# Adapter stage of a two-layer adapter network: base weight split in sixteen halves at the end of a step, and y copied ahead of the second half of the next x

## The reference, cut to what matters

```python
# x: (64, 64, 1024), two layers
x = x + L0_ffn(einsum('bct,bcd->bdt', x, W0[id0]))          # layer 0
def L1_cond(x, weight, ids):                                 # one of 16 adapters for each of 64 batches
    return einsum('bij,bkj->bik', x, weight[ids])            # y = x @ weight[id].T, 1024 x 1024
def L1_ffn(y):
    base_out = einsum('bsi,oi->bso', y, base_w) + base_b     # the base weight, 1024 x 1024
    res_hidden = einsum('bsi,ri->bsr', y, A)                 # rank 64
    # router over 16 experts, the best two, gates from a softmax
    delta = einsum('bse,bsr,eor->bso', combine, res_hidden, B)
    return base_out + 0.5 * delta
x = x + L1_ffn(L1_cond(x, L1_cond_weight, id1))              # layer 1
```

## Time and profile before

| | us |
|---|---|
| median of 3 runs | 1214.57 |
| lowest and highest | 1213.8, 1217.22 |
| profiled execution, its own time | 1211.74 |
| its span | 1210.1 |
| PE busy, DVE busy, ACT busy, POOL busy | 1115.4, 689.7, 504.9, 221.0 |
| granted PE clock, mean | 0.977 |

### The profile page before, as it was taken

The page is one execution under the profiler, slowest core; times in us unless marked ns, Lnnn a source line. Parts: engine busy times, 40 slices in busy tenths (PEclk is TensorE's granted clock), DMA queues, the critical chain, the costliest instruction groups (busy, mean ns, idle before and its releaser), DMA issues.

```text
span 1210.1 us, 22388 instructions
## 1 busy us (share of the span) xinstructions
PE 1115.4 (92%) x5799; PEld 921.9 (76%) x5800; DVE 689.7 (57%) x1307; ACT 504.9 (42%) x1019; POOL 221.0 (18%) x352
## 2 busy tenths in 40 slices
PE   4989969988999899999999899989999899999997
PEld 4979958867888677777887778767676678888885
DVE  2877863472554728364555386735444366666655
ACT  1101213562654638363556471134444344444443
POOL 1021110020110202010111000054444042323220
PEclk8989979998999999999999999999999999999998
DMA  5488764493573828475665333169999799999995
GB/s 203 162 325 279 268 237 128 129 319 129 183 267 105 323 77 306 134 250 193 215 222 189 124 98 104 64 220 363 369 351 282 280 377 353 341 355 336 358 344 202
DMA packets 115051, 289.38 MB, mean 239 GB/s; under 512 B 17202, under 2 KB 21810, under 8 KB 112946
## 3 DMA queue, kind: packets, MB, share of 16 engines
q1 hardware_dynamic: 85088, 184.91, 42.9%
q0 software_dynamic: 29056, 102.38, 25.5%
q10 hardware_dynamic: 850, 1.39, 0.4%
HBM read 184.79 MB, written 103.84 MB: 239 GB/s over the span
## 4 chain that ended last, share of the span: by engine, by line
PE 65%; DVE 13%; DMA 9%; issue 7%; ACT 3%; SPq 2%; DVEq 1%; ACTq 1%; another core or an unknown queue 0%; POOLq 0%; POOL 0%
PE psum L1344 14%; PE psum L1346 14%; PE psum L1345 14%; PE psum L1529 3%; PE psum L1428 3%; DMA delta_scratch<-dl 2%; PE psum L1530 2%; PE psum L1420 2%; PE psum L1538 2%; PE psum L1355 2%; PE psum L1446 2%; DMA xp<-act_scratch 2%; PE psum L1448 2%; DMA rawb<-baseT 2%; DVE x1g L985 2%
## 5 line engine op out<-in xcount | busy, mean ns | idle before, releaser
L1344 PE MATMUL psum<-base_hi,xp_hi 128*128 128x512 f32 x512 | 204.2, 399 | 2.5 <-ACT nat L757 1.5
L1344 PE MATMUL psum<-w,xp_hi 128*128 128x512 f32 x448 | 185.5, 414 | 19.8 <-DVE xp_lo L1035 17.2
L1345 PE MATMUL psum<-base_lo,xp_hi 128*128 128x512 f32 x512 | 200.8, 392 | 0.0
L1346 PE MATMUL psum<-base_hi,xp_lo 128*128 128x512 f32 x512 | 200.7, 392 | 0.0
L1346 PE MATMUL psum<-w,xp_lo 128*128 128x512 f32 x448 | 180.0, 402 | 0.0
L1345 PE MATMUL psum<-w,xp_hi 128*128 128x512 f32 x448 | 179.8, 401 | 0.0
L583 POOL DMA_DIRECT2D raw<-w1T x112 | 59.3, 529 | 461.8 <-DVE w L1014 461.3
L1014 DVE TENSOR_TENSOR w<-raw,w 128x1024 fp32r<-128x1024 f32 x112 | 132.1, 1218 | 5.5 <-ACT w L696 3.5
L749 ACT ACTIVATE xp_hi<-xp 128x256 fp32r<-128x256 f32 x124 | 51.4, 416 | 179.4 <-PE psum L1346 137.8
L1116 DVE TENSOR_TENSOR xp_lo<-xp,xp_hi 128x256 fp32r<-128x256 f32 x124 | 51.9, 424 | 117.9 <-ACT xp_hi L749 95.2
L1344 PEld LDWEIGHTS psum<-w,xp_hi 128*128 128x128 f32 x448 | 85.7, 191 | 42.6 <-issue 24.8
(11 more groups left out here) (263 smaller groups left out, 1912.6 us busy)
## 6 DMA issues: line engine op xcount, KB each, us to landing
raw<-w1T POOLq DMA_DIRECT2D x120, 512.0 KB, 5.6
delta_scratch<-dl SPq DMA_DIRECT2D x80, 512.0 KB
xp<-act_scratch SPq DMA_DIRECT2D x74, 256.0 KB, 2.8
act_scratch<-yT SPq DMA_DIRECT2D x72, 256.0 KB, 4.7
xg<-xT SPq DMA_DIRECT2D x16, 1024.0 KB, 7.4
act_scratch<-x1g SPq DMA_DIRECT2D x16, 1024.0 KB, 5.1
x1t<-act_scratch SPq DMA_DIRECT2D x64, 256.0 KB
out<-x1t SPq DMA_DIRECT2D x64, 256.0 KB
```

The lines of the kernel that those rows point to most:

```text
L1344: mm(out, a_hi, b_hi, start=start, stop=False, skip_group_check=True)
L1345: mm(out, a_hi, b_lo, start=False, stop=False, skip_group_check=True)
L1346: return mm(out, a_lo, b_hi, start=False, stop=stop, skip_group_check=True)
```

## The change

The buffer `rawb` becomes two parts of 512 columns. The base weight comes in sixteen halves (`PARTS` = 2 KC = 16, `HALF` = 512 columns), one in each of steps 0 to 15. Part n goes to home n % 2. On ACT and DVE the base split moves from ahead of the first half of the next x to the end of the step, behind weight chunks 6 and 7. The copy of y moves ahead of the second half of the next x on both engines. SP's wait for `base_lo_done` now is for the part before the last one, and it also waits for the last part to have landed.

```diff
-            rawb = sb(s, "rawb", [P, D])
+            rawb = sb(s, "rawb", [P, 2, HALF])
@@ SP
-            sp.dma_start(rawb[:, :], baseT[0, :, :]).then_inc(rawb_in, 16)
+            sp.dma_start(rawb[:, 0, :], baseT[0, :, 0:HALF]).then_inc(rawb_in, 16)
...
                 load_pair(j + 2)
-                with sp.If(j < KC - 1):
-                    chunk = baseT[bass.ds(nc.s_assert_within(j + 1, 1, KC - 1), 1), :, :].rearrange("a p d -> p (a d)")
-                    sp.wait_ge(base_lo_done, j + 2)
-                    sp.dma_start(rawb[:, :], chunk).then_inc(rawb_in, 16)
+                with sp.If(j < PARTS - 1):
+                    n = nc.s_assert_within(j + 1, 1, PARTS - 1)
+                    part = baseT[bass.ds(n // 2, 1), :, bass.ds(n % 2 * HALF, HALF)].rearrange("a p d -> p (a d)")
+                    home = rawb[:, bass.ds(n % 2, 1), :].rearrange("p a d -> p (a d)")
+                    sp.wait_ge(rawb_in, j * 16 + 16)
+                    sp.wait_ge(base_lo_done, j + 1)
+                    sp.dma_start(home, part).then_inc(rawb_in, 16)
                 store_pair(j)
@@ ACT, step
                 w_chunks(range(2, KC // 2))
-                base_high(j)
                 act.wait_ge(mm_done, KC * j + KC // 2)
                 x_high(j + 1, 0)
                 w_chunks(range(KC // 2, LATE))
                 rh_part(j)
                 act.wait_ge(mm_done, KC * j + KC)
-                x_high(j + 1, 1)
                 with act.If(j == lone):
                     y_copy(j, True)
                 with act.Else():
                     y_copy(j, False)
+                x_high(j + 1, 1)
                 w_chunks(range(LATE, KC))
+                base_high(j)
@@ DVE, step
                 low_chunks(range(2, KC // 2))
-                base_low(j)
                 one = alone(dve, j + 1)
                 x_low(j + 1, 0, one)
                 low_chunks(range(KC // 2, LATE))
                 rh_sum(j)
-                x_low(j + 1, 1, one)
                 with dve.If(j == lone):
                     y_copy(j, True)
                 with dve.Else():
                     y_copy(j, False)
+                x_low(j + 1, 1, one)
                 low_chunks(range(LATE, KC))
+                base_low(j)
@@ PE
-            pe.wait_ge(base_lo_done, KC + 1)
+            pe.wait_ge(base_lo_done, PARTS + 1)
```

More of the change, by code:

```diff
@@ L43 @@
 HRING = 8
+HALF = D // 2
+PARTS = 2 * KC
 T_LOAD, T_STORE, T_ADAPTER = 0, SLOTS, 2 * SLOTS
@@ L678, in base_high @@
             def base_high(j):
-                with act.If(j < KC):
-                    chunk = base_hi[:, bass.ds(nc.s_assert_within(j, 0, KC - 1), 1), :].rearrange("p a d -> p (a d)")
+                with act.If(j < PARTS):
+                    n = nc.s_assert_within(j, 0, PARTS - 1)
+                    part = base_hi[:, :, :].rearrange("p k d -> p (k d)")[:, bass.ds(n * HALF, HALF)]
+                    home = rawb[:, bass.ds(n % 2, 1), :].rearrange("p a d -> p (a d)")
                     act.wait_ge(rawb_in, 16 * j + 16)
-                    act.activation(chunk, rawb[:, :], ACT.Copy).then_inc(base_hi_done, 1)
+                    act.activation(part, home, ACT.Copy).then_inc(base_hi_done, 1)
             def rh_part(v):
@@ L1057, in base_low @@
             def base_low(j):
-                with dve.If(j < KC):
-                    i = bass.ds(nc.s_assert_within(j, 0, KC - 1), 1)
+                with dve.If(j < PARTS):
+                    n = nc.s_assert_within(j, 0, PARTS - 1)
+                    low, high = (b[:, :, :].rearrange("p k d -> p (k d)")[:, bass.ds(n * HALF, HALF)]
+                                 for b in (base_lo, base_hi))
+                    home = rawb[:, bass.ds(n % 2, 1), :].rearrange("p a d -> p (a d)")
                     dve.wait_ge(base_hi_done, j + 1)
-                    tt(base_lo[:, i, :].rearrange("p a d -> p (a d)"), rawb[:, :],
-                       base_hi[:, i, :].rearrange("p a d -> p (a d)").bitcast(F32), ALU.subtract
-                       ).then_inc(base_lo_done, 1)
+                    tt(low, home, high.bitcast(F32), ALU.subtract).then_inc(base_lo_done, 1)
             def rh_sum(v):
```

## The result

| | before | after |
|---|---|---|
| median, 7 runs of each, us | 1214.57 | 1205.57 |
| lowest and highest, us | 1208.37, 1217.32 | 1202.71, 1213.12 |
| profiled execution, its span, us | 1211.74, 1210.1 | 1204.83, 1203.2 |

The ratio of the two is 0.9942 with a 95% interval of 0.9914 to 0.9969: about 7 us (3.8 to 10.4) faster, where 17.3 us were forecast. The time lies in the range given, but above the forecast's own 1193.5 to 1203. The change does what it was expected to do for the first ten steps; in the next six it is slower than the kernel before.

A forecast was written before the change was run, and what follows sets the result against it. PE was taken to bound the adapter stage, so only its idle time and lost clock could be won. Base part 11.9 plus copies 6.1 less edge cost 0.7 gave 17.3 us, 1197.3 us against the 1214.57 median; range 1192.5 to 1207.

The forecast's parts named there:

- The base part, 11.9 us: Adapter steps 0 to 7: moving and halving the base split wins 7.1 us of gaps plus 4.8 us of clock.
- All three gaps: PE's waits for the next x's low part in base-split steps, 0.73, 3.20 and 3.18 us, expected to go.
- the 0.6 of step 5: Step 5's share of the kept gains from copying y first: 0.6 us less PE wait for the turn.
- Of the twelve gaps I count as kept those not followed by such a bound ... together 6.1 us: PE's waits to turn y: copying y first wins 6.1 us where neither DVE nor next x binds; bounds 2 to 11.
- A half behind step 14 makes that longer by 0.69 us. Bounds 0 and 1.4: PE's 1.69 us wait in step 15 for the turned y's split grows; 0.7 us taken as cost.
- the copies' 1.5 us: Kept gains from copying y first between turns 10 and 16: step 14 1.0 us, step 16 0.5 us.
- SP's share, costed at nothing: SP's eight more base loads and two waits cost 0 us, bounds 0 and 0.5; each part ordered a step ahead.
- the wait for the low x: Sign of being right: PE's wait in the stage falls from 17.2 to 10 us or less.
- Rival 1: Copies of y win nothing because DVE or the next x takes it back: 11.2 us won, 1203.4 us; chance 0.20.
- Rival 2: All copy gaps won and x ordered earlier, so late-x gaps go too: 23 us won, 1191.6 us; chance 0.07.
- Rival 3: Base loads beside weight reloads in steps 8 to 15 stretch x's landing: 5 to 11 us left, about 1207; chance 0.09.
- Rival 4: Base part lands after its step's end, stopping PE at rank products in steps 0 to 15: about 1236 us; chance 0.04.

The follow-up runs named there:

- e3: The changed kernel run again for the spread; ratio to the kernel before 0.9930.
- e15: The changed kernel run a third time; ratio to the kernel before 0.9948, median 1202.71 us.
- e4: The kernel before run again for the spread; ratio 1.0001.
- e10: The kernel before, with only SP ordering the loads of x and base ahead of the rank store, whole chunks and old split place; ratio 0.9913.
- e13: The kernel before with y copied first and only the base load ordered ahead of the rank store, x at its old time; ratio to before 0.9895.
- e2: The kernel before with only the copies of y moved ahead of the second half of x; ratio to before 0.9947.
- e1: The changed kernel with the copies of y back behind the second half of x, so the base part alone; ratio to before 0.9931.
- e6: The changed kernel with base halves only in steps without weight work, none in an edge, parts ordered two ahead; ratio to before 0.9917.
- e8: e6 with the copies of y behind the second half of x; ratio to the kernel before 0.9937.
- e7: The changed kernel with SP ordering the loads of x and base ahead of the rank store; ratio to the kernel before 0.9891.
- e11: e7 with the second half of x ahead of the copies of y; ratio to the kernel before 0.9921.
- e12: e10 with the copies of y first; ratio to the kernel before 0.9868.
- e14: e12 run again beside e15; ratio to the kernel before 0.9859, median 1190.66 us.
- e9: e6 with the load of x alone ordered ahead of the rank store; ratio to the kernel before 0.9878.
- e5: The changed kernel with the sixteen halves split at the old place, ahead of the first half of next x; ratio to before 1.0017.

## Why the prediction was right and wrong

Forecast 17.3 us, measured 9.0 by the two medians, 7.0 by the ratio, and 8.5 and 6.3 by the ratios of the two repetitions (e3, e15). Three terms make the sum, and the runs give each a size of its own (medians, by ratios to before; a difference of two ratios is uncertain by some 3 to 4 us, so these are sizes and no more).

**The base part, 11.9 us: right where it acts, and at the upper end in size.** All three gaps are gone, the clock is 1.00 in both stretches, and ACT's wait for rawb is nil. The lead at turn 10 is 12.9 us, less 0.6 at the start 12.3, where this term and the 0.6 of step 5 make 12.5. Against the second profile of before (e4) it is 9.6 us. There the three gaps were as large (0.48, 3.90 and 3.08 us), but the clock fell behind the first long one only (0.83 from 260 to 270 us, 1.00 from 280 to 290), so the 3.1 us of clock behind the second were chance in the one profile that I read. The term is worth 9 to 12 us. The cause that I gave, ACT held for a late load, is shown by e10 and, apart from x, by e13. That the split had to be moved for it is not: the time of the order was enough.

**"Of the twelve gaps I count as kept those not followed by such a bound ... together 6.1 us": the step that failed most.** The gaps themselves go as told: steps 3 and 13 fell from 14.11 us each to 12.97 and 12.96, and the waits for the turn from 13.0 to 3.8 us. At the stage's end 1.91 us are left, and not 1.3. Alone the copies win 6.4 us (e2 to before). Beside the base part they win 0.8 at most (e3 to e1). The waits say what takes it back: behind the earlier turn PE waits at the rank product for DVE's split, 8.2 us where e1 has 4.2, and for a late x, 5.1, 1.4 and 3.2 us where e1 has none (in its one profile, its fastest execution). The edits agree. The copies win 2.4 us with the halves out of the edges (e6 to e8) and 3.6 with the loads ordered earlier (e7 to e11), neither of them clear of noise, and 5.4 and 6.5, which is, with both (the halves gone altogether; e12 and e14 to e10). So both bounds that I had named, DVE and the next x, bind more gaps beside the base part than I had counted. In the profiles of the change steps 20 and 21 take 15.1 to 15.4 and 14.9 to 16.5 us, which are 14.0 and 13.9 in e1; x was late at step 21 in the first profile of before too, and not in the second (15.84 and 14.14 us), so this differs from one execution to the next. I had judged each gap by what stood behind it in a trace in which the other half of the change was missing. That a faster step leaves less time between the order of x, which hangs on the rank result, and its use would explain the late x; no run shows this by itself.

**"A half behind step 14 makes that longer by 0.69 us. Bounds 0 and 1.4": mis-sized.** The halves at edges cost 1.6 to 3 us by the ratios (e6 to the change, e9 to e7), where I took 0.7. The profile says why. A half costs 0.8 to 1.0 us at an edge and not 0.69, since I counted the operation and not the idle time of the block around it. It stands at every edge up to step 15, and I counted one: step 10 grew from 14.37 to 15.61 us, 0.8 of it by the half (15.20 in e1) and 0.4 by the copies (14.79 in e2). Above all I put no clock on this term, though I had put 4.8 us of clock on the gaps of the term before it. The wait in step 15 grew from 1.69 to 3.05 us, and the clock behind it fell in all four profiles that have 3.05 us (after, e3, e15, e7), which is 0.34 x 10 = 3.4 us in the window shown. It fell behind the shorter gaps of e4 and e10, too, so how much of the 3.4 us belongs to the longer gap is open. With the copies' 1.5 us, the forecast for turns 10 to 16 was a gain of 0.8 us; the profiles show 86.9, 86.9 and 89.9 us against 82.7 and 83.7. SP's share, costed at nothing, held: ACT never waited for a part. The lead that I gave for it, a whole step or some 14 us, was wrong in its reading: a part is ordered early in the step at whose end it is used, and the lead is 9.4 to 17.3 us. It was enough against landings of up to 7.1 us.

**The signs.** Of the signs named, ACT's wait, the sixteen operations, the wait for the turn and the growing wait in step 15 came as told. Two did not: the wait for the low x is 13.3 us in the first profile (9.6 and 10.6 in e3 and e15) and not 10 or less, and the clock did not stay at 1.00.

**The rivals.** Rival 1, 11.2 us and 1203.4, was nearly right, in time and in mechanism: the copies win next to nothing beside the base part, because DVE and the next x take it back. It had a chance of 0.20. Rival 2's further gain from x ordered sooner did not come; x is late in two to four steps in all three profiles of the change. Rival 3 has the right price and the wrong cause (e7). Rival 4, the base part late at its step's end, never happened: ACT never waited for it. By the Trainium skill, DMA: Bandwidth & Descriptors, its rule on batching in section Bandwidth and its fixed cost in Anatomy of one DMA, the prediction estimated that about 1 us would be left of the gain. The runs don't bear this out for the change, which won some 7. Where ACT waits for the halves, eight more of them did cost 8.5 us (e5 against e2); where nobody waits for them, as in the change, no such cost was seen.

**What stays open.** In e7 turns 16 to 36 are 4 to 7 us shorter than in the change, and the late x itself explains 1.4 to 5.1 of it; waits for the high part of a lone pair's x have another 0.7, 1.2 and 1.6 us, and where the rest lies I did not follow. Which edge half costs what was not tried one by one. Nor can the clock's share of the loss in step 15 be told in whole times, since the runs of one kernel spread by up to 1%.

## What to carry to other kernels

When an engine waits for a load, look first at what stands ahead of that load in its queue's program; ordering it ahead of a wait that it doesn't need cost nothing that these runs show, while moving or cutting the work can land it where the engine has no cover. Price a gap that grows with the clock that may fall behind it, also when it is one's own side effect. And a gain in a stage with two or three near bounds isn't a sum of gaps: remove the next bound first, then count.

## What was unexpected of the hardware

The clock does not answer to a gap alone. Windows of 390 to 400 us in e1 and e11, where PE met the same gap of 2.52 us in step 15:

```profile
390.00:400.00 10.00, 7.34 (x39) 5.67 (x39) 9.05 (x11) 7.85 (x12) 3.06 (x6) 1.00 0.92 308
```

```profile
390.00:400.00 10.00, 7.48 (x28) 6.36 (x27) 8.95 (x11) 5.51 (x8) 3.18 (x6) 0.66 1.01 376
```

At gaps of 1.7 to 2.2 us in step 15 it fell behind them in e8, e10 and e13, for a shorter stretch in e9, e14 and the second profile of before (e4: 0.83 from 400 to 410 us), and not in e2, e6, e12 and the first profile of before. In e15 it fell at another place too, behind a stop of 1.45 us near 325.7, and that step took 18.74 us instead of 15.61. So one profile can't price a clock loss within 3 us: it takes several.

A base load's landing has two sizes. In the kernel after, five of the sixteen halves, ordered in steps 5, 6, 10, 11 and 15, landed after 5.9 to 7.1 us, and the others after 2.9 to 3.3; in the kernel before, the chunks ordered in steps 5 and 6 took 7.5 and 7.8 us, and the fastest 3.4. While a late half was on its way the DMA engines were busy with weight reloads too, at a share of 0.86 to 1.03 (249 to 257, 264 to 270, 319 to 326 and 335 to 342 us), against 0.62 and 0.64 for two early ones (289 to 293, 303 to 307 us). For the late ones half the bytes made little difference. The load of x ordered earlier (e7) lands in 4.0 us at the median instead of 2.8, and is on time all the same.
